# A transformer block on eight cores: row maxima taken inside the first feed-forward product, and the first score product split by bank

## What is computed

```
x = x + layernorm(attn(layernorm(x)))
x = x + layernorm(ffn(layernorm(x)))

attn:  q, k, v = x @ W_qkv           # 16 heads of 64
       k = layernorm(k)              # within each head
       linear attention, causal, in chunks: scores (q k^T, masked) @ v + S @ q,
       S = S + v^T k                 # carried along the sequence
       @ W_o
ffn:   h = layernorm(x)
       h = qlinear(h, w1)            # rows scaled by 127 / max|h|, rounded; weights rounded to -1, 0, 1
       h = gelu(h)
       h = qlinear(h, w2)
```

## Time and profile before

| | us |
|---|---|
| median of 2 runs | 3634.64 (3634.21 to 3635.07) |
| the profiled execution, its own time | 3630.47 |
| span of its slowest core (core 6) | 3628.9 |
| spans of the eight cores | 3598.7 to 3628.9 |
| busy on that core: PE / VectorE / ScalarE | 2127.5 / 1538.3 / 723.1 |
| mean granted TensorE clock | 0.771 of full speed |

### The profile page before, as it was taken

The page is one execution under the profiler, slowest core; times in us unless marked ns, Lnnn a source line. Parts: engine busy times, 40 slices in busy tenths (PEclk is TensorE's granted clock), DMA queues, the critical chain, the costliest instruction groups (busy, mean ns, idle before and its releaser), DMA issues.

```text
span 3628.9 us, 33891 instructions; the slowest of 8 cores (3598.7 to 3628.9 us)
## 1 busy us (share of the span) xinstructions
PE 2127.5 (59%) x10640; PEld 1042.9 (29%) x10640; DVE 1538.3 (42%) x2492; ACT 723.1 (20%) x1193; POOL 146.2 (4%) x203
## 2 busy tenths in 40 slices
PE   0151567647665376747675376657565467576665
PEld 0141444412222143412222244322222244222222
DVE  0576543455353134355443244364533243453542
ACT  0031321222221122122121122122221121122211
POOL 0141300000000000000000000000000000000000
PEclk9999666668878667678887676688787666688777
DMA  9897911131011311131111311131101311211111
GB/s 193 245 207 233 156 27 27 27 110 35 21 41 32 128 27 27 24 113 33 29 32 38 125 25 31 26 111 27 41 21 38 125 33 27 96 44 27 35 30 41
DMA packets 333137, 245.50 MB, mean 68 GB/s; under 512 B 304272, under 2 KB 304288, under 8 KB 328864
## 3 DMA queue, kind: packets, MB, share of 16 engines
q0 software_dynamic: 97440, 184.58, 18.1%
q1 hardware_dynamic: 235520, 58.74, 8.6%
HBM read 159.41 MB, written 33.55 MB: 53 GB/s over the span
## 4 chain that ended last, share of the span: by engine, by line
PE 38%; DVE 22%; DMA 19%; ACT 9%; issue 8%; DVEq 3%; another core or an unknown queue 0%; SPq 0%; ACTq 0%; POOL 0%; POOLq 0%; PEldq 0%; PEld 0%
PE pb L989 13%; PE pb L906 10%; DMA abf<-abf 6%; PE pb L492 5%; DMA af<-x 4%; DMA af<-w 4%; PE pb L499 3%; DMA w2q_t<-w2qs 3%; DVE af L950 2%; DVE abf L954 2%; DVEq L206 2%; PE pb L909 2%; ACT af L917 1%; DMA wqkv_t<-w_qkv 1%; DVE abf L576 1%
## 5 line engine op out<-in xcount | busy, mean ns | idle before, releaser
L906 PE MATMUL pb<-w1q_t,abf 128*128 128x512 fp8e4 x2048 | 573.1, 430 | 459.6 <-DMA abf<-abf 318.5
L989 PE MATMUL pb<-w2q_t,abf 128*128 128x512 fp8e4 x2048 | 481.8, 396 | 78.0 <-ACT s2rowr L978 44.4
L906 PEld LDWEIGHTS pb<-w1q_t,abf 128*128 128x128 bf16 x2048 | 197.4, 106 | 759.4 <-issue 619.0
L492 PE MATMUL pb<-abf,wqkv_t 128*128 128x128 bf16 x2048 | 198.8, 290 | 250.4 <-DMA abf<-abf 250.4
L989 PEld LDWEIGHTS pb<-w2q_t,abf 128*128 128x128 bf16 x2048 | 202.7, 101 | 339.5 <-issue 130.0
L1022 DVE RECIPROCAL scal<-scal 128x1 f32<-128x1 f32 x32 | 5.3, 164 | 670.7 <-ACT scal L1018 670.7
L492 PEld LDWEIGHTS pb<-abf,wqkv_t 128*128 128x128 bf16 x2048 | 194.1, 137 | 254.3 <-issue 254.3
L917 ACT ACTIVATE af<-pb,scal 128x512 f32<-128x512 f32 x256 | 159.9, 685 | 260.7 <-PE pb L909 241.4
L528 DVE TENSOR_REDUCE khs<-pb 128x8 f32<-128x512 f32 x32 | 22.1, 692 | 439.9 <-ACT af L509 439.9
L925 DVE TENSOR_REDUCE khs<-af 128x1 f32<-128x1024 f32 x128 | 156.2, 1220 | 86.2 <-ACT af L917 50.9
L294 DVE TENSOR_REDUCE af<-af 128x1 f32<-128x4096 f32 x16 | 70.7, 4420 | 146.2 <-DMA af<-w 146.2
(11 more groups left out here) (162 smaller groups left out, 2710.6 us busy)
## 6 DMA issues: line engine op xcount, KB each, us to landing
af<-w POOLq DMA_DIRECT2D x16, 2048.0 KB, 9.7
wqkv_t<-qkvs POOLq DMA_DIRECT2D x3, 6144.0 KB, 20.4
af<-w POOLq DMA_DIRECT2D x32, 512.0 KB, 5.2
af<-w POOLq DMA_DIRECT2D x16, 1024.0 KB, 9.0
af<-x POOLq DMA_DIRECT2D x32, 512.0 KB, 3.9
w1q_t<-w1qs POOLq DMA_DIRECT2D x4, 4096.0 KB, 13.9
w2q_t<-w2qs POOLq DMA_DIRECT2D x4, 4096.0 KB, 23.1
out<-x POOLq DMA_DIRECT2D x32, 512.0 KB, 2.9
```

The lines of the kernel that those rows point to most:

```text
L492: mi = PE.matmul(pq, lhsT=wqkv[:, kk, m * 128:(m + 1) * 128], rhs=hf[:, kk, :], start=(kk == 0), stop=(kk == 7))
L906: PE.matmul(Bk[bb0 + n2][:, :], lhsT=xf[:, kk, :], rhs=w1q[:, kk, hs0:hs0 + 512], start=(kk == 0), stop=False)
L989: mi = PE.matmul(Bk[4 + n2][:, :], lhsT=xq2_fm[:, kk, :], rhs=w2q[:, kk, n2 * 512:n2 * 512 + 512], start=(kk == 0), stop=False)
```

## The change

Two edits.

1. In attention, the first eight score matmuls are split: the four even heads (bank 4) are issued first and wait only for the activation L733 that reads bank 4 (a new count, `ac_ln2a0`), then the four odd heads (bank 5), which wait for L736 as before.
2. In the feed-forward part, the four maxima over `g_sb` move from `f_q2(gg)` into the slab loop of `f_f1(gg)`, each right behind its slab's Gelu. Since `f_f1(gg+1)` stands ahead of `f_tail(gg-1)` in the loop, the maxima of a tile now stand ahead of the tail that used to be ahead of them.

```
@@ a_sc
             if gg >= 1:
+                PE.wait_ge(s_ac, ms[f"ac_ln2a0_{seg}_{gg-1}"])
+            for h in (0, 2, 4, 6):
+                mi = PE.matmul(Bk[4][:, (h // 2) * 128:(h // 2) * 128 + 128],
+                               lhsT=kf[0:64, h // 2, :],
+                               rhs=qfm[0:64, h // 2, :],
+                               start=True, stop=True, tile_position=(0, 0),
+                               skip_group_check=True)
+            if gg >= 1:
                 PE.wait_ge(s_ac, ms[f"ac_ln2a_{seg}_{gg-1}"])
-            for h in range(8):
-                par = h % 2
-                mi = PE.matmul(Bk[4 + par][:, (h // 2) * 128:(h // 2) * 128 + 128],
-                               lhsT=kf[par * 64:par * 64 + 64, h // 2, :],
...
+            for h in (1, 3, 5, 7):
+                mi = PE.matmul(Bk[5][:, (h // 2) * 128:(h // 2) * 128 + 128],
+                               lhsT=kf[64:128, h // 2, :],
...
@@ a_ln2
-            A.activation(out=tmpa[:, 0:512], in_=Bk[4][:], func=AF.Identity,
...
+            ai = A.activation(out=tmpa[:, 0:512], in_=Bk[4][:], func=AF.Identity,
...
+            ac_mark(ai); ms[f"ac_ln2a0_{seg}_{gg}"] = cnt["ac"]
@@ f_f1, f_q2
                 ac_mark(ai); ms[f"ac_gel_{seg}_{gg}_{slab}"] = cnt["ac"]
-
-        def f_q2(gg):
-            r = gg % 4
-            for slab in range(4):
                 V.wait_ge(s_ac, ms[f"ac_gel_{seg}_{gg}_{slab}"])
                 vo(f"qp{slab}", [], lambda slab=slab: V.tensor_reduce(
                     out=khs[:, r, 60 + slab:61 + slab],
                     in_=g_sb[:, slab * 1024:(slab + 1) * 1024],
                     axis=AX.X, op=ALU.max, apply_absolute_value=True))
+
+        def f_q2(gg):
+            r = gg % 4
             vo("qm2", ["qp0", "qp1", "qp2", "qp3"], lambda: V.tensor_reduce(
```

More of the change, by code:

```diff
@@ L608, in a_sc @@
             if gg >= 1:
-                PE.wait_ge(s_ac, ms[f"ac_ln2a_{seg}_{gg-1}"])
-            for h in range(8):
-                par = h % 2
-                mi = PE.matmul(Bk[4 + par][:, (h // 2) * 128:(h // 2) * 128 + 128],
-                               lhsT=kf[par * 64:par * 64 + 64, h // 2, :],
-                               rhs=qfm[par * 64:par * 64 + 64, h // 2, :],
-                               start=True, stop=True, tile_position=(par * 64, 0),
+                PE.wait_ge(s_ac, ms[f"ac_ln2a0_{seg}_{gg-1}"])
[6 more added lines that the diff above has]
+            if gg >= 1:
+                PE.wait_ge(s_ac, ms[f"ac_ln2a_{seg}_{gg-1}"])
+            for h in (1, 3, 5, 7):
+                mi = PE.matmul(Bk[5][:, (h // 2) * 128:(h // 2) * 128 + 128],
+                               lhsT=kf[64:128, h // 2, :],
+                               rhs=qfm[64:128, h // 2, :],
+                               start=True, stop=True, tile_position=(64, 0),
                                skip_group_check=True)
@@ L732, in a_ln2 @@
             A.wait_ge(s_dv, ms[f"dv_ln2r_{seg}_{gg}"])
-            A.activation(out=tmpa[:, 0:512], in_=Bk[4][:], func=AF.Identity,
-                         scale=scal[:, r, SL_R2:SL_R2 + 1],
-                         bias=scal[:, r, SL_B2:SL_B2 + 1])
+            ai = A.activation(out=tmpa[:, 0:512], in_=Bk[4][:], func=AF.Identity,
+                              scale=scal[:, r, SL_R2:SL_R2 + 1],
+                              bias=scal[:, r, SL_B2:SL_B2 + 1])
+            ac_mark(ai); ms[f"ac_ln2a0_{seg}_{gg}"] = cnt["ac"]
             ai = A.activation(out=tmpa[:, 512:1024], in_=Bk[5][:], func=AF.Identity,
```

## The result

| | before | after |
|---|---|---|
| median | 3643.61 us (3634.16 to 3653.94, 8 runs) | 3527.93 us (3517.77 to 3530.16, 9 runs) |
| ratio | 1 | **0.9679** (95% interval 0.9661 to 0.9697) |
| span of the slowest core in the profile | 3628.9 us | 3521.2 us |
| mean granted clock on that core | 0.771 | 0.776 |

The change makes the kernel 3.2% faster. Predicted were 3520 us from 3634.6, a ratio of 0.9685. The difference of the medians is 115.7 us, predicted were 115. (Both medians lie above what the prediction started from or named: the kernel before by 9 us against its first two runs, the changed kernel by 8 us against the forecast.

What follows compares the result with a forecast made beforehand. No engine was taken as the bound: work passes between engines, so a step is worth what it holds up. Terms 114 + 21 - 20 + 0 = 115 us off 3634.6 gave 3520 us, range 3493 to 3554.

Steps and rivals of the forecast that it cites:

- The maxima in tiles 3 to 6: Feed-forward: scale starts 5.19 us earlier, removing the slab 2 stall and slow matmuls; 7.1 x 16 = 114 us saved.
- What is late next: Tile start: it hangs on add, store and transpose, so the 13.2 us stall before each tile stays whole.
- The clock of the second product: Second product: behind an unbroken first product the 1.60 us stop lowers the clock; 12 tiles lose 1.69, 20 us lost.
- The rival that the clock stays up: Second product: no 20 us lost and four slow tiles recover; 142 us saved, 3493 us; chance 0.13.
- the one that it is held down: Second product: denser work keeps TensorE at the low clock throughout; 197 us more, 3717 us; chance 0.03.
- The segment ends: Behind each segment's last second product the maxima lie wholly on the path; 4 x 5.19 = 21 us saved.
- The moved maxima cost nothing: VectorE behind the Gelus: the second product covers the moved maxima with 14 us to spare; without cover, 3.3 us per tile.
- The scores: Attention: even heads may start 0.7 us earlier, but the residual add delays the mask anyway; 0 us taken.
- the bound of the gain: Attention scores: at most 4 us gained, half of 0.3 us in 28 tiles.
- The held quantization: Rival: quantization waits for the next tile's transpose, only segment ends gain; 3614 us; chance 0.08, shared with similar waits.
- The sum: Whole kernel: 114 + 21 - 20 + 0 = 115 us saved.

Runs made afterwards that it cites:

- The transpose issued ahead: The changed kernel with the transpose of the tile after next issued ahead of the store of the tail: 3507.38 us, ratio 0.9603 to the kernel before.
- early tail: The changed kernel with the tail of the tile before moved ahead of the second product's matmuls: 3160.82 us, ratio 0.8653 to the kernel before.
- short fill: The changed kernel with seven unused matmuls filling TensorE's 1.6 us wait for the scales before the second product: 3500.03 us, ratio 0.9585 to the kernel before.

## Why the prediction was right

**The maxima in tiles 3 to 6 (114 us).** Right, and by its mechanism. The 16 tiles take 21.40 us from tile start to second product in the mean (21.10 to 21.71), as tile 7 had shown beforehand with 21.39; before it was 28.64. Saved: 7.24 x 16 = 116 us. The rest wait in slab 2 is 1.6 us in all. That the maxima's place and nothing else did this is shown by the second edit alone, which has the whole gain, and by the doubled maxima: 95 us in the old place, none that could be measured in the new.

**What is late next.** The tile start stood still, as predicted: 13.2 to 13.8 us of idle PE before each. The transpose issued ahead shows how near the two chains lie: with one of them shortened, the tile keeps its 51.4 us.

**The clock of the second product (-20 us).** 13 of the 16 second products are slow now; 4 were before. 9 x 1.69 = 15 us, where I had counted 12 new ones. On the other cores 12 to 14 of the 16 are slow. That it takes the 1.6 us stop is shown by its fill; that behind an unbroken first product the stop nearly always does it was taken from eight cases and held, without a reason that any run shows. The rival that the clock stays up was wrong; so was the one that it is held down.

**The segment ends (21 us).** The idle time before the last scale transpose fell from 54.2 to 32.9 us over four segments, 21.3 us.

**The moved maxima cost nothing.** Right: the scale still waits 16.7 us, and 12.4 us with twice the maxima.

**The scores (0 us).** Right, alone too: 0.9991 with 1 inside the interval. Regrouping the heads lengthened the eight matmuls from 0.61 to 1.25 us from first start to last end, with a gap of only 0.09 between the halves, and the residual add covers it. Each half alone takes 0.58 us for four matmuls, nearly what eight took by turns, at the same granted clock of 0.50. The Trainium skill ("TensorEngine Tiling (Array Packing)", "Tiling Modes") lets one expect that matmuls of one row group lose their overlap, and the trace agrees with these 0.58 us. The 0.3 us per tile behind the bound of the gain has no row; it did not enter the sum.

**The held quantization.** This rival is refuted: L957 starts 5.2 us earlier against the add, and in the row above its 0.19 us are put down to "issue".

**The sum.** 116 + 21 - 15 = 122 us. The feed-forward parts, from the first tile start to the start of the last second product, shrank by 28.5, 31.9, 29.6 and 29.8 us, together 119.8. The span shrank by only 107.7: some 12 us were lost outside the feed-forward parts. On this core some 20 were lost at the two places of each segment where weights are loaded (9.4 of them are TensorE's longer idle time before the four tiles 0), and 10 came back in attention, which differs by 7 to 8 us from core to core in either kernel. At the loads, the page's DMA issues of the changed kernel (KB each, median us to landing) show

```profile
wqkv_t<-qkvs POOLq DMA_DIRECT2D x3, 6144.0 KB, 23.6
...
w2q_t<-w2qs POOLq DMA_DIRECT2D x4, 4096.0 KB, 26.0
```

where the profile of the kernel before had 20.4 and 23.1. The change is not the cause: the kernel before with the maxima doubled in their old place, which has neither edit, shows 24.4 and 26.6. Over the twelve traces these loads take 20.4 to 25.4 and 23.1 to 27.6 us. What sets them was not tried.

So the profile of the kernel before happens to be one of its shorter executions (3630 us, where the median is 3644), and the medians compare more fairly: 115.7 us, with some 7 to either side. That this meets the forecast of 115 to within 1 us is luck. The terms that came true add up to 122, 7 more than I had summed, 5 of them from the clock; what took them back lies within the scatter of the runs.

## What to carry to other kernels

Work on an engine is worth what stands behind it, so before making an instruction faster look whether it can stand elsewhere in that engine's order: a reduction put behind a late step cost 5 us a tile (and some 2 us of slow matmuls behind the stall), and nothing once it stood ahead of it. Where two chains run from one event, find the event: shortening either chain ends at the other, while moving the event (here the tail's square root, stuck behind the second product on ScalarE) gave three times as much as the change itself. And a removed stall must be priced with the clock: it brings back the slow matmuls behind it, and may make the next stop the one in which the clock falls. Last, where parts of the program scatter by themselves, as the loads of the weights do here, compare the stretch that was changed in the traces, besides the whole time.

## What I had not expected of the hardware

- A stop of 1.6 us between two dense stretches can be enough for the clock to fall to its 1.2 GHz level: in 13 of 16 tiles here, and in 8 of 8 of the unbroken ones before. With that stop filled, every second product behind a first one ran at full speed, on all eight cores. But it does not always happen: before tiles 1 and 2 a stop of 1.54 us never did it in the changed kernel, on any core, and before the tile starts of tiles 3 to 7 of the early tail a stop of the same 1.6 us did it in 0 to 5 of 20 cases, by core. The length of the stop does not decide alone.
- With two such stops per tile the slow stretch moves in part: with one filled, some 10 of 20 tile starts had slow first matmuls (2.4 to 3.4 us for eight in the trace shown, where 1.89 is full speed), and no gain showed in the time (ratio 0.8677 against 0.8653 without the fill).
- Many more matmuls on all eight cores (2353 instead of 2120 us of busy PE) did not hold the clock down: the second products ran at full speed. They were not free all the same: the 56 matmuls before the tile start made the feed-forward parts 10 us longer than the short fill alone, through the wait in slab 2.
